# Cross attention with a router: who writes the residual base, and how the rank threshold is found

## The reference

```python
x = x + self_attention(layernorm(x))                 # 16 heads of 64, with the 128 best-scored keys added
x = x + cross_attention(ctx, ctx, layernorm(x))      # 16 heads of 32 over 77 context rows, no output product
x = x + routed(layernorm(x))                         # 64 rows of each batch are chosen
```

```python
weights = (y @ router_w)[..., 0] + router_b[0]
topv, topi = top_k(weights, 64)                      # int(0.125 * 512) = 64
sel_mask = (weights > topv[:, -1])                   # the 63 rows above the 64th weight
sel_idx = sort(topi[:, :63])                         # these go through attention and a feed-forward
out = zeros.at[sel_idx].set(processed)
x = x + out + y * (1 - sel_mask)
```

## Time and profile before

| | |
|---|---|
| time, median of 3 runs | 2294.71 us (2288.63 to 2298.39) |
| the profiled execution | 2289.59 us, span 2287.9 us |
| PE busy | 2112.8 us, 92% of the span |
| PE weight loads busy | 1651.3 us, 72% |
| DVE busy | 1333.4 us, 58% |
| ACT busy | 837.5 us, 37% |
| POOL busy | 697.9 us, 31% |
| granted clock of PE, mean | 0.947 of full speed |

### The profile page before, as it was taken

The page is one execution under the profiler, slowest core; times in us unless marked ns, Lnnn a source line. Parts: engine busy times, 40 slices in busy tenths (PEclk is TensorE's granted clock), DMA queues, the critical chain, the costliest instruction groups (busy, mean ns, idle before and its releaser), DMA issues. The chain is left out here.

```text
span 2287.9 us, 36708 instructions
## 1 busy us (share of the span) xinstructions
PE 2112.8 (92%) x12029; PEld 1651.3 (72%) x12029; DVE 1333.4 (58%) x3141; ACT 837.5 (37%) x1537; POOL 697.9 (31%) x1060
## 2 busy tenths in 40 slices
PE   4999999999999999999999999987899999878899
PEld 4886886788688688678768858855788888854443
DVE  3673485277178268447627817734887878745401
ACT  2442443344144144234324414414544444313210
POOL 4320321131142042122113113215776767520000
PEclk9999999999999999999999999997887879769899
DMA  4101101100200211111011011012013212150000
GB/s 138 38 29 58 37 29 33 61 29 29 65 29 29 66 29 37 33 51 38 25 60 38 25 60 38 29 56 63 27 59 132 67 49 67 51 202 0 1 0 19
DMA packets 112665, 110.13 MB, mean 48 GB/s; under 512 B 12083, under 2 KB 78643, under 8 KB 111976
## 3 DMA queue, kind: packets, MB, share of 16 engines
q1 hardware_dynamic: 111848, 105.74, 14.6%
q0 software_dynamic: 640, 2.10, 0.2%
HBM read 89.99 MB, written 17.83 MB: 47 GB/s over the span
## 5 line engine op out<-in xcount | busy, mean ns | idle before, releaser
L338 POOL TENSOR_TENSOR idle<-ones 128x4 f32<-128x4 f32 x171 | 36.1, 211 | 1129.8 <-PE pj_bank L607 812.2
L438 ACT ACTIVATE probs<-s_bank,nmax 128x512 f32<-128x512 f32 (+3 forms) x512 | 249.6, 526 | 346.5 <-DVE nmax L558 245.0
L708 PE MATMUL o_bank<-vals,probs_t 128*128 128x65 f32 x2560 | 323.0, 269 | 0.0
L708 PEld LDWEIGHTS o_bank<-vals,probs_t 128*128 128x128 f32 x2560 | 311.0, 192 | 3.3 <-DVE probs_t L566 3.3
L558 DVE TENSOR_REDUCE nmax<-s_bank 128x1 f32<-128x512 f32 (+2 forms) x384 | 184.4, 508 | 199.2 <-PE s_bank L685 195.7
L732 PE MATMUL pj_bank<-w_o,o_t 128*128 128x512 f32 x512 | 226.9, 604 | 6.0 <-ACT o_t L446 6.0
L566 DVE COPY probs_t<-pt_bank 128x512 f32<-128x512 f32 x320 | 217.7, 680 | 3.6 <-PE pt_bank L693 3.6
L693 PE MATMUL pt_bank<-ident,probs 128*128 128x128 f32 x1280 | 194.8, 275 | 14.6 <-DVE probs_t L566 14.4
L732 PEld LDWEIGHTS pj_bank<-w_o,o_t 128*128 128x128 f32 x512 | 98.3, 193 | 129.9 <-issue 129.9
L681 PE MATMUL s_bank<-k_twice,q_both 128*128 128x512 f32 (+3 forms) x512 | 189.5, 372 | 0.0
L416 ACT ACTIVATE vals<-pj_bank,twice 128x512 f32<-128x512 f32 x64 | 44.0, 688 | 350.9 <-PE pj_bank L607 338.2
(11 more groups left out here) (263 smaller groups left out, 4427.2 us busy)
## 6 DMA issues: line engine op xcount, KB each, us to landing
wq_raw<-in_L_attn_w_q SPq DMA_DIRECT2D x65, 256.0 KB, 3.0
wk_raw<-in_L_attn_w_k SPq DMA_DIRECT2D x65, 256.0 KB, 3.8
xb<-in_x SPq DMA_DIRECT2D x9, 1024.0 KB, 5.5
xt<-x SPq DMA_DIRECT2D x36, 256.0 KB, 2.8
probs<-in_x SPq DMA_DIRECT2D x32, 256.0 KB, 2.7
x<-probs SPq DMA_DIRECT2D x32, 256.0 KB, 2.0
am<-in_L_ffn_attention_mask SPq DMA_DIRECT2D x8, 1024.0 KB, 5.4
out<-x SPq DMA_DIRECT2D x32, 256.0 KB, 2.1
```

The lines of the kernel that those rows point to most:

```text
L438: ins = nc.scalar.activation(probs[:, i % 2, c0:c0 + nk], s_bank[i % 2][:, c0:c0 + nk], ACT.Exp, bias=nmax[:, i % 4, n:n + 1])
L708: ins = nc.tensor.matmul(o_bank[slot][:, o0:o0 + VW], probs_t[:, i % 2, c0 + P * kt:c0 + P * kt + P], vals[:, kt, 2 * p + h, :], start=(kt ...
```

## The change

- `base` goes from DVE to ACT, in the form `x2 = x2 * (1 + stay * rs) + stay * nb`, since y is `x2 * rs + nb`. It reads `x2` alone and two numbers for each row from the new tile `on_base`. It moves one slot later (20 and 21).
- So that rs and nb of batch n-2 are still there, the second set of `scales` becomes `scales2` with one buffer for each parity.
- The third pass of each rank (L1194) and the step from it to `stay` (L1199) go. In their place comes `last` in slot 19, after `t` and before `e` on PE: four accumulated matmuls of 128x128 by one column, which put the weight of rank 63 on all partitions into the last column of `r_bank[0]`. `last_take`, at the end of DVE's slot 19, compares it with the weights (`stay`), multiplies rs and nb by it and adds 1: three tiny steps, then `on_base_ready`.
- `row_take` goes. The two passes that are left read the row from PSUM, in `r_bank[1]`; the first of them waits for `row_ready`.
- PE's wait for `sel` is now in `last`, and its first `a1` waits for `on_base_ready` too.

```diff
-    at += [("dot", t, 2 * t + 9) for t in range(TT)] + [("row", 0, 15), ("row_take", 0, 16)]
+    at += [("dot", t, 2 * t + 9) for t in range(TT)] + [("row", 0, 15)]
     at += [("rank", t, (16, 16, 17, 18)[t]) for t in range(TT)] + [("pick", 0, 18)]
-    at += [("base", t, 19 + t // 2) for t in range(TT)] + [("xs", c, 19 + (c + 1) // 2) for c in range(DC)]
+    at += [("last", 0, 19), ("last_take", 0, 19)]
+    at += [("base", t, 20 + t // 2) for t in range(TT)] + [("xs", c, 19 + (c + 1) // 2) for c in range(DC)]
     at += [("a1", c, 21 + c // 2) for c in range(TT)] + [("xs_take", 0, 22), ("a1_take", 0, 23)]
-    order = ("turn", "xl", "e_take", "pv_take", "t", "max", "xs_take", "norm", "xl2", "dot", "row_take",
-             "rank", "pick", "e", "pv", "row", "ctx", "base", "xs", "a1", "a1_take", "stats")
+    order = ("turn", "xl", "e_take", "pv_take", "t", "max", "xs_take", "norm", "xl2", "dot",
+             "rank", "pick", "last", "e", "pv", "row", "ctx", "base", "xs", "a1", "a1_take", "last_take", "stats")
...
+                if kind == "base":
+                    act.wait_ge(on_base_ready, n.count(1, 1))
+                    nc.scalar.activation(x2[:, n.par, i, :], x2[:, n.par, i, :], ACT.Identity,
+                                         bias=on_base[:, n.par, 1, i:i + 1], scale=on_base[:, n.par, 0, i:i + 1]
+                                         ).then_inc(base_ready, 1)
...
-                if kind == "row_take":
-                    dv.wait_ge(row_ready, n.count(1, 1))
-                    nc.vector.tensor_copy(row_s[:, :], r_bank[1][:, :]).then_inc(row_copied, 1)
-                    dv.wait_ge(row_copied, n.count(1, 1))
                 if kind == "rank":
 
                     w = info[:, n.par, i, 0:1]
+                    if i == 0:
+                        dv.wait_ge(row_ready, n.count(1, 1))
                     done.wait(dv)
                     y0 = P * (TT - 1 - i)
-                    step(nc.vector.tensor_scalar(junk[:, :], row_s[:, :], w, None, ALU.is_gt, ALU.add,
+                    step(nc.vector.tensor_scalar(junk[:, :], r_bank[1][:, :], w, None, ALU.is_gt, ALU.add,
                                                  accum_out=cnt[:, 0, i:i + 1]))
-                    step(nc.vector.scalar_tensor_tensor(junk[:, :], row_s[:, :], w, before[:, y0:y0 + S],
+                    step(nc.vector.scalar_tensor_tensor(junk[:, :], r_bank[1][:, :], w, before[:, y0:y0 + S],
                                                         ALU.is_equal, ALU.mult, accum_out=cnt[:, 1, i:i + 1]))
-                    step(nc.vector.tensor_scalar(junk[:, :], row_s[:, :], w, None, ALU.is_ge, ALU.add,
-                                                 accum_out=cnt[:, 2, i:i + 1]))
                 if kind == "pick":
                     step(nc.vector.tensor_tensor(cnt[:, 0, :], cnt[:, 0, :], cnt[:, 1, :], ALU.add))
-
-                    step(nc.vector.tensor_scalar(stay[:, :], cnt[:, 2, :], KEEP - 0.5, None, ALU.is_gt))
...
-                if kind == "base":
-                    rows = x2[:, n.par, i, :]
-                    nc.vector.scalar_tensor_tensor(rows, xl2[:, n.par, i, :], stay[:, i:i + 1], rows, ALU.mult,
-                                                   ALU.add).then_inc(base_ready, 1)
+                if kind == "last_take":
+
+                    dv.wait_ge(last_ready, n.count(1, 1))
+                    step(nc.vector.tensor_scalar(stay[:, :], info[:, n.par, :, 0], r_bank[0][:, LAST:LAST + 1], None,
+                                                 ALU.is_le))
+                    step(nc.vector.tensor_tensor(on_base[:, n.par], scales2[:, n.par, RS:NB + 1:NB - RS, :],
+                                                 stay[:, :].unsqueeze(1).broadcast_to((P, 2, TT)), ALU.mult))
+                    nc.vector.tensor_scalar(on_base[:, n.par, 0, :], on_base[:, n.par, 0, :], 1.0, None,
+                                            ALU.add).then_inc(on_base_ready, 1)
...
+                if kind == "last":
+                    pe.wait_ge(sel_ready, n.count(1, 1))
+                    for t in range(TT):
+                        ins = nc.tensor.matmul(r_bank[0][:, LAST:LAST + 1],
+                                               info[:, n.par, t, 0:1].broadcast_to((P, P)), sel[:, t, KEEP - 1:KEEP],
+                                               start=(t == 0), stop=(t == TT - 1))
+                    ins.then_inc(last_ready, 1)
...
                 if kind == "a1":
                     if i == 0:
                         pe.wait_ge(am_in, n.count(16, 16))
+                        pe.wait_ge(on_base_ready, n.count(1, 1))
```

More of the change, by code:

```diff
@@ L746 @@
 SLOTS = 2 * TT
+LAST = S - 1
 class Batch:
@@ L846, in cross_and_router @@
         xl2 = sb("xl2", [P, 2, TT, D])
-        row_s = sb("x_row_s", [P, S])
         junk = sb("x_junk", [P, S], BF16)
@@ L853, in cross_and_router @@
         idle_v, at_start = sb("idle_v", [P, 2]), sb("at_start", [P, 2 * TT])
-        scales = sb("scales", [P, 2, 3, TT])
+        scales, scales2 = sb("scales", [P, 3, TT]), sb("scales2", [P, 2, 3, TT])
+        on_base = sb("on_base", [P, 2, 2, TT])
         RS, NM, NB = range(3)
         info = sb("info", [P, 2, TT, 3])
-        cnt = sb("x_cnt", [P, 3, TT])
+        cnt = sb("x_cnt", [P, 2, TT])
         stay = sb("stay", [P, TT])
@@ L875, in cross_and_router @@
             sem(n) for n in ("x_pt_ready", "pt_copied", "x_pv_ready", "att_ready", "x2_ready"))
-        stats2_ready, xl2_ready, info_ready, row_ready, row_copied, sel_ready = (
-            sem(n) for n in ("stats2_ready", "xl2_ready", "info_ready", "row_ready", "x_row_copied", "sel_ready"))
+        stats2_ready, xl2_ready, info_ready, row_ready, sel_ready, last_ready, on_base_ready = (
+            sem(n) for n in ("stats2_ready", "xl2_ready", "info_ready", "row_ready", "sel_ready", "last_ready",
+                             "on_base_ready"))
         xs_ready, a1_ready, xs_copied, a1_copied, base_ready = (
@@ L1025, in step, with scale @@
                 done.wait(pl)
-            def scale(r, tiles, ready):
-                rs, nm, nb = (scales[:, r, k, tiles] for k in (RS, NM, NB))
+            def scale(to, r, tiles, ready):
+                rs, nm, nb = (to[:, k, tiles] for k in (RS, NM, NB))
                 step(nc.gpsimd.tensor_tensor(rs, mv[:, r, tiles, 1], eps_ln[:, tiles], ALU.add))
@@ L1037, in work @@
                     pl.wait_ge(stats_ready, n.count(1, 1))
-                    scale(0, slice(0, TT), scales_ready)
+                    scale(scales, 0, slice(0, TT), scales_ready)
                 if kind == "e_take":
@@ L1054, in work @@
                     pl.wait_ge(stats2_ready, n.count(TT, i + 1))
-                    scale(1, slice(i, i + 1), scales2_ready)
+                    scale(scales2[:, n.par], 1, slice(i, i + 1), scales2_ready)
             run(work, pl, done, 2 * 3 * (1 + TT))
@@ L1087, in work @@
                     nc.scalar.activation(xl[:, i % 2, :], xt[:, n.par, i, :], ACT.Identity,
-                                         bias=scales[:, 0, NB, i:i + 1], scale=scales[:, 0, RS, i:i + 1]
+                                         bias=scales[:, NB, i:i + 1], scale=scales[:, RS, i:i + 1]
                                          ).then_inc(xl_ready, 1)
@@ L1108, in work @@
                     nc.scalar.activation(xl2[:, n.par, i, :], x2[:, n.par, i, :], ACT.Identity,
-                                         bias=scales[:, 1, NB, i:i + 1], scale=scales[:, 1, RS, i:i + 1]
+                                         bias=scales2[:, n.par, NB, i:i + 1], scale=scales2[:, n.par, RS, i:i + 1]
                                          ).then_inc(xl2_ready, 1)
+                if kind == "base":
[3 more added lines that the diff above has]
+                                         ).then_inc(base_ready, 1)
             run(work, act)
@@ L1216, in work @@
                                             ALU.mult).then_inc(a1_copied, 1)
-                if kind == "base":
-                    rows = x2[:, n.par, i, :]
-                    nc.vector.scalar_tensor_tensor(rows, xl2[:, n.par, i, :], stay[:, i:i + 1], rows, ALU.mult,
-                                                   ALU.add).then_inc(base_ready, 1)
+                if kind == "last_take":
[6 more added lines that the diff above has]
+                                            ALU.add).then_inc(on_base_ready, 1)
             for k, at_one in enumerate((*base_out[0], *base_out[1])):
                 nc.vector.memset(at_start[:, k:k + 1], 0.0).then_inc(at_one, 1)
-            run(work, dv, done, 2 * (TT + HALVES + TT + TT + 1 + 3 * TT + 2))
+            run(work, dv, done, 2 * (TT + HALVES + TT + TT + 1 + 2 * TT + 1 + 2))
         @block.tensor
@@ L1291, in work @@
                     ins.then_inc(row_ready, 1)
+                if kind == "last":
[5 more added lines that the diff above has]
+                    ins.then_inc(last_ready, 1)
                 if kind == "xs":
-                    if i == 0:
```

(1 more changed line is left out.)

## The result

The changed kernel takes 2268.32 us (median of 4 runs, 2263.48 to 2270.38) against 2293.59 for the kernel before (2288.63 to 2298.39): 25.3 us less, a ratio of 0.9886 with a 95% interval of 0.9870 to 0.9903. The profiled execution took 2263.48 us, its span is 2261.6 us, 26.3 less than before.

A forecast was written before the change was run, and what follows sets the result against it. DVE sets slots 0 to 2 and PE the rest, taking turns. Gains of 13.5 + 10.5 + 2.6 + 3.1 = 29.7, so 30 us, against the median of 2294.7 give 2265 us, range 2246 to 2284.

The forecast's parts named there:

- the odd periods: Three periods behind the loop's end: PE, without any pause, gets its clock back in part; 3.5 us gained each, 10.5 together.
- the stall: Slot 7 with the loop's end, 12.16 us against 6.7 without it: taken as given, no gain counted.
- three even periods, loop's end aside: Periods behind no loop's end: 4.1 us from slots 0 to 2, 0.4 from slots 3 to 7; 4.5 each, 13.5 together.
- drain and last batch: End of the stage, where PE waits for DVE: 2.6 us gained in the drain, 3.1 in the last batch.
- Slots 0 to 2: DVE sets these slots and loses 4.1 us a period there; slots near 6.5, 6.0 and 5.6 us.
- Passes from PSUM: DVE's two remaining rank passes, reading the row from PSUM: 0 us taken, at most 0.1 us gained a pass.
- The base: Moved to ScalarE, slots 4 and 5: worth nothing by itself, passes hidden; its later store holds POOL some 2.5 us longer.
- The last clause of the prediction: Sign of being wrong: POOL's first addition of slot 5 is released by a store, and PE's `t` by that.
- The cover of 2 us: Slot 5: time left before PE needs ScalarE's exponential, after POOL stands 2.5 us longer for the store; cost 0.
- `last`: PE in slot 3: four weight loads and one-column products, costing 0.5 us a period, between 0.4 and 0.9.
- The clock returns everywhere: Rival, chance 0.15: nothing drops PE's clock; 6.6 us in three periods, 7.8 in three, 2246 us in all.
- PE eats it: Rival, chance 0.12: PE's clock stays as now; 3.5 us gained in three periods, 0.5 to 1 in three; 2279 us.

The follow-up runs named there:

- run 1: The kernel before with only the ranks reading the row from PSUM, its copy dropped: 2282.50 us, ratio 0.9976 [0.9941, 1.0010].
- run 5: The changed kernel with SyncE issuing all four loads of the next x before the four stores of the base: 2268.75 us, ratio 0.9897.
- run 2: The kernel before with only the residual base moved to ScalarE, stores one slot later: 2286.35 us, ratio 0.9971 [0.9958, 0.9985].
- Run 10: The changed kernel with the threshold by one product instead of four, and two tiny DVE instructions more: 2253.49 us, ratio 0.9827.
- run 4: The changed kernel with 20 one-column memsets filling DVE's loop body to its old 304 instructions: 2269.63 us, ratio 0.9903.
- run 9: The changed kernel with six idle PE products a batch, four in slot 1 and two in slot 2: 2251.69 us, ratio 0.9824.
- run 12: The changed kernel with the threshold by one product and eight idle PE products a batch in slots 1 to 3: 2243.53 us, ratio 0.9797.
- run 8: The changed kernel with four idle PE products a batch in slot 1, read by nobody: 2263.65 us, ratio 0.9876 [0.9852, 0.9899].

## Why the prediction was right, and where it was not

The forecast was 2265 us with 30 us of gain; measured were 2268.3 and 25.3, 26.3 by the profiles. That the sum came so close is in part luck, as its terms show: the odd periods missed theirs by 16 us, and the stall, put at 0, gave 11.5.

| term | forecast | measured |
|---|---|---|
| three even periods, loop's end aside | 13.5 | 5.1 + 2.6 + 5.2 = 12.9 |
| stall at the loop's end | 0 | 6.0 + 5.5 = 11.5 |
| three odd periods | 10.5 | -2.2 - 1.6 - 1.8 = -5.5 |
| drain and last batch | 5.7 | 4.6 |
| ahead of the whole periods | 0 | 3.5 |
| behind the stage | 0 | -0.6 |

*Slots 0 to 2.* Right: 22.04 - 18.21 = 3.8 us for 4.1, with slots of 6.41, 5.91 and 5.89 for 6.5, 6.0 and 5.6. DVE is busy 16.6 of these 18.2 us, so it still sets them. PE's longest wait for the masking is 1.3 us, not under 1, and the clock of slots 1 to 4 is 0.86 and 0.71, not over 0.8 throughout.

*Passes from PSUM.* Right: 0 more, by run 1 too.

*The base.* Right that its ScalarE passes (806 ns) are hidden and that the store comes to hold POOL, by 2.7 to 3.2 us for 2.5. The cover of 2 us held: no idle moment of PE in slots 5 and 6 is over 0.24 us. The last clause of the prediction took a release of POOL by a store as a sign of being wrong only with PE's `t` held by it, and that didn't come. The wait of DVE for the fourth load of x, which the prediction named and didn't price, is hidden as well (run 5). By itself, the move gained 0.3% (run 2), which the prediction put at nothing.

*`last`.* Mis-sized, 0.5 us for 0.95 at full and 1.7 to 1.86 at half clock, because I counted four records where these fp32 products make eight. In the last batch it stands open:

```profile
1986.63 1.86 PE L1301 MATMUL r_bank<-sel,info 128*128 128x1 f32 x8 [7.66 <-DVE sel L1203]
```

From the row's transposes to the gather there are 1988.36 - 1977.91 = 10.45 us for 12.78 before: 2.3 gained for 3.1 forecast. In the odd periods it lies in slot 3, at half clock, where PE has no pause. Run 10 gave back 13.5 to 14.8 us by taking most of it away, where the sum had set aside 0.5 to 1.0 us a batch.

*The odd periods.* This is the step that failed: "if the clock comes back as early as in the other parity [...] I take 3.5, a little above the middle". The time went up instead. The reason given, that PE would be without any pause, was false for slots 1 and 2, where PE at full clock is faster than DVE and idles 2.2 and 0.85 us. The half speed that follows lies on slots 2 to 4, and PE fills 3 and 4. Before, in the two odd periods behind a return, the clock was at 0.50 to 0.54 throughout slots 0 to 2, where half speed costs little since DVE sets the pace, and it was back at 1.00 in slot 4. Runs 4, 9 and 12 move the fall: the odd periods take 55.5 us with slots 2 to 4 at half speed, 52.2 with the stall and a fall in slot 3, and 48.7 with none.

*The loop's end.* The prediction took its 5.5 to 6 us as given. It went with the shorter body, and by itself gave nothing that can be told: run 4 has it back in the same time. So the rows +11.5 and -5.5 of the table belong together: without the stall the clock's fall lands in another place.

*Rivals.* "The clock returns everywhere" put a period at 46.1 us. The change alone didn't reach that: its best are 47.5. Nor did run 12, where the clock is at 1.00 in four periods and a cheaper threshold is in: these take 47.5 to 48.7. "PE eats it" describes the odd periods, which lost 1.6 to 2.2 us where it gave them 0.5 to 1.

## What to carry to other kernels

When an engine that paces the others gets faster, ask how long TensorE now stands idle in those stretches (here 2.2 us in slot 1) and which full stretch comes next: at 2.4 GHz it idles more, and half speed costs where it is full (here 15.45 us for 8.17 in slots 3 and 4). A stall that goes is no gain until it is put back alone and the time is seen to rise. Four small products that broadcast a value cost by their number and not by their columns (1.46 us a batch for four of one column, 0.44 for one of four), so fold them into one, and count the records of such an fp32 product as two.

## What the runs showed of the hardware

- Products of TensorE's that nobody reads can pay: with six a batch, run 9 is 16.6 us faster than the changed kernel by the medians (0.9824 against 0.9886, the intervals apart). With eight a batch, run 12 spends 39.6 us of recorded products on them in all. The Trainium skill, "TensorE: Matmul & The Clock Gate" (A second HAM failure mode), tells of short idle moments between groups that make the clock go up and down; the traces here agree in that the clock falls behind slots in which PE idles for 2.16 us in sum (changed kernel, slot 1) or 0.56 (run 8, slot 1 of the period from 1839.83), but it also held behind 1.62 (run 9).
- DVE's loop went back in no visible time with bodies of 284 and 286 instructions, and with 5.8 to 6.5 us of standing with 302 and 304. Where between these the limit lies wasn't tried.
- Four loads of a broadcast column with one-column products take 1.7 to 1.86 us at 1.2 GHz and 0.95 at 2.4, eight records of each.
- Why the clock falls in slot 2 in the odd periods and recovers in the even ones, with nearly the same idle time of 2.16 and 2.19 us ahead of it, stays open. The odd ones have a slot 1 that is 1.2 us longer. The DMA isn't it: its share in slots 0 and 1 is 1.03 and 1.06 in the period from 1733.83, 0.64 and 0.00 in that from 1839.37, and the clock falls in both.
